# The last copy to the output, by every second row instead of by halves

## The reference, cut to what matters

```
x = x + gnn(layernorm(x), edges, ...)          # x is [2500, 512] float32
x = x + ffn(layernorm(x)[None], ...)[0]

# in ffn:
for e in range(8):
    h = gelu(xf @ W1[e] + b1[e])
    y = h @ W2[e] + b2[e]
    out = out + comb[:, e:e+1] * y             # comb is zero but for a row's two experts
```

## Time and profile before

| | |
|---|---|
| median of 3 runs | 868.01 us (867.37 to 868.9) |
| the profiled execution's own time | 863.36 us |
| its span, first to last instruction | 861.7 us |
| last copy issued (both queues) | 842.8 us |
| from issue to landing, the two transfers | 16.7 and 18.4 us |
| copied | 5.12 MB |

### The profile page before, as it was taken

The page is one execution under the profiler, slowest core; times in us unless marked ns, Lnnn a source line. Parts: engine busy times, 40 slices in busy tenths (PEclk is TensorE's granted clock), DMA queues, the critical chain, the costliest instruction groups (busy, mean ns, idle before and its releaser), DMA issues.

```text
span 861.7 us, 14833 instructions
## 1 busy us (share of the span) xinstructions
PE 696.6 (81%) x3260; PEld 553.6 (64%) x3261; DVE 457.2 (53%) x1232; ACT 415.4 (48%) x1134; POOL 457.3 (53%) x530
## 2 busy tenths in 40 slices
PE   4999355879888787879788888959889999999960
PEld 3777245657766666667676767845547787888840
DVE  5998223555555555556465555668485433333320
ACT  4443442545545554536455545618754444545430
POOL 5000575666666666666666666310105677777750
PEclk9999687998989899989999898988988999999995
DMA  5342576666666666666656666407993577777768
GB/s 197 117 155 92 156 213 164 172 188 168 186 181 174 178 177 182 186 171 183 189 166 184 176 179 179 118 27 283 334 380 127 104 131 131 135 131 135 130 91 250
DMA packets 58299, 146.96 MB, mean 171 GB/s; under 512 B 8868, under 2 KB 18708, under 8 KB 57880
## 3 DMA queue, kind: packets, MB, share of 16 engines
q0 software_dynamic: 35216, 106.84, 50.6%
q1 hardware_dynamic: 22968, 37.16, 12.3%
q10 hardware_dynamic: 80, 2.56, 1.0%
HBM read 118.17 MB, written 33.47 MB: 176 GB/s over the span
## 4 chain that ended last, share of the span: by engine, by line
PE 40%; issue 19%; DVE 11%; DMA 11%; ACT 4%; POOL 4%; POOLq 2%; DVEq 2%; another core or an unknown queue 2%; ACTq 1%; SPq 1%
PE ps L705 30%; DMA result<-y,si 8%; PE ps L659 3%; POOL rows L506 2%; DMA x_all<-in_x_dram 2%; ACT E L951 2%; ACT ps L951 2%; PE ps L844 1%; DVE Wt L1217 1%; PE ps L785 1%; DVE S L1228 1%; DVE acc L1235 1%; PE ps L755 1%; POOL xg L593 1%
## 5 line engine op out<-in xcount | busy, mean ns | idle before, releaser
L705 PE MATMUL ps<-rows,S 128*128 128x257 f32 x1556 | 383.4, 404 | 98.7 <-issue 83.9
L506 POOL DMA_INDIRECT rows<-node_table,srcT x313 | 301.8, 964 | 234.4 <-issue 83.8
L705 PEld LDWEIGHTS ps<-rows,S 128*128 128x128 f32 x1556 | 312.3, 202 | 169.6 <-issue 121.3
L951 ACT ACTIVATE E<-sdst_b,rows 128x128 f32 x389 | 124.0, 389 | 236.2 <-DVE Wt L1217 120.7
L1235 DVE TENSOR_TENSOR acc<-acc,ps 128x514 f32 x99 | 68.0, 687 | 116.1 <-remote 77.6
L1228 DVE SCALAR_TENSOR_TENSOR S<-ps,lane,Wt 128x128 f32<-128x128 f32 x389 | 109.6, 345 | 4.4 <-issue 0.8
L951 ACT ACTIVATE ps<-sdst_b,rows 128x128 f32 x313 | 96.2, 351 | 2.0 <-issue 2.0
L844 PE MATMUL ps<-W_e,xgT 128*128 x352 | 83.4, 380 | 0.0
L602 POOL DMA_INDIRECT result<-y,si x44 | 70.4, 1601 | 11.4 <-issue 7.1
L1222 DVE TENSOR_TENSOR lane<-dstT,node_id 128x4 f32 (+1 forms) x98 | 16.1, 164 | 111.5 <-issue 77.0
L844 PEld LDWEIGHTS ps<-W_e,xgT 128*128 128x128 f32 x352 | 63.4, 190 | 6.9
(11 more groups left out here) (203 smaller groups left out, 678.8 us busy)
## 6 DMA issues: line engine op xcount, KB each, us to landing
W_e<-in_L_ffn_W_dram SPq DMA_DIRECT2D x16, 512.0 KB, 8.5
node_table<-rows SPq DMA_DIRECT2D x20, 258.0 KB, 2.7
result<-acc SPq DMA_DIRECT2D x20, 256.0 KB, 2.5
xn_table<-xn SPq DMA_DIRECT2D x20, 256.0 KB, 2.2
rows<-node_table,srcT POOLq DMA_INDIRECT x313
x_all<-in_x_dram SPq DMA_DIRECT2D x19, 256.0 KB, 3.1
out_dram<-result SPq DMA_DIRECT2D x1, 2500.0 KB, 16.7
out_dram<-result ACTq DMA_DIRECT2D x1, 2500.0 KB, 18.4
```

Source lines behind the costliest of these rows:

```text
L506: nc.gpsimd.indirect_dma_start(out=rows[:, g % RING, c, :], out_offset=None, in_=table, in_offset=bass.IndirectOffsetOnAxis(ap=srcT[:, GC ...
L705: m = pe.matmul(ps_agg[q][:, a, 0:HALF], S[:, w, c, :], rows[:, r, c, a * HALF:(a + 1) * HALF], start=(c == 0), stop=(c == n - 1))
L951: m = nc.scalar.activation(e[:, c, :], sdst_b[:, bass.ds(tile * P, P)], ACT.Exp, bias=bias, scale=scale)
```

## The change

Both transfers still copy 1250 rows each, on the same queues, at the same place, behind the same waits. Before, SyncE copied rows 0 to 1249 and ScalarE rows 1250 to 2499. Now SyncE copies the even rows and ScalarE the odd ones, on both sides. A new helper makes the view, and an assert says that the number of rows is even.

```
+        def in_turn(t, half):
+
+            return t[0:N, :].rearrange("(r two) d -> two r d", two=2)[half]
...
-            sp.dma_start(out[0:N // 2, :], result[0:N // 2, :]).then_inc(st_out, 16)
+            sp.dma_start(in_turn(out, 0), in_turn(result, 0)).then_inc(st_out, 16)
...
-            act.dma_start(out[N // 2:N, :], result[N // 2:N, :]).then_inc(st_out, 16)
+            act.dma_start(in_turn(out, 1), in_turn(result, 1)).then_inc(st_out, 16)
```

More of the change, by code:

```diff
@@ L108, in gnn_moe_kernel @@
         rows = sg("rows", [P, RING, GC, ROW], F32, first)
-        assert layer_end <= top[0]
+        assert layer_end <= top[0] and N % 2 == 0
         before = top[0]
```

## The result

The changed kernel takes 874.03 us (median of 4, 873.22 to 875.84) against 867.85 us of the kernel before on the same chip (median of 4): a ratio of 1.0071, 95% interval [1.0045, 1.0096], 6.2 us slower, with 3.9 to 8.3 us as the interval. Both intervals hold the 4.9 us that the traces show in the copy itself.

What follows compares the result with a forecast made beforehand. The exposed output copy at the end was taken to decide any change: 1.3 us to first byte, 23.0 moving and 0.4 at the end make 24.7 against 18.4, so 868.0 + 6.3 = 874.3 us, range 871.0 to 880.0.

Steps and rivals of the forecast that it cites:

- The copy is wholly exposed: Output copy at the kernel's end: nothing computes beside it, so its 18.4 us, longer or shorter, changes kernel time in full.
- Ten engines, by the divisor: Output copy: 1250 rows per queue run on ten engines instead of 16, 10 being the largest divisor up to 16.
- 250 packets of 92 ns, 23.0 us: Moving time of the output copy: each shared engine carries 250 row packets at 92 ns, 23.0 us.
- The pieces given to a queue, at nothing: Output copy: 2500 pieces instead of 128 cost nothing, at 340 pieces a microsecond; at most 3.7 us for one queue.
- Issue to first byte, 1.3 us: Start of the output copy: 1.3 us from its issue until the first packet moves.
- Gaps of 0.4 us: End of the output copy: uneven finish and the way to the semaphore shrink from 1.3 to 0.4 us.
- The sum: Output copy from issue to landing: 24.7 us against 18.4, so the kernel is 6.3 us slower.
- Sixteen engines and faster: Rival for the output copy: pieces dealt to all 16 engines at a load's pace, 3.4 us sooner, 864.6 us; 7%.
- Its counterpart, memory or something else shared as the limit: Rival for the output copy: sixteen engines, but memory limits at 299 GB/s, no change, 867.2 to 868.5 us; 5%.
- Packets that wait for reading and writing in turn: Rival for the output copy: ten engines, 110 to 178 ns a packet, up to 27.8 us more, 895.8 us; 9%.
- Two engines by a power of two: Rival for the output copy: only two engines per copy, 1250 packets on each, 88 us more; 1%.

Runs made afterwards that it cites:

- long-piece kernel: Against the kernel before: the two queues copy alternate pieces of 51,200 bytes, 50 each, on ten engines; ratio 1.0047 [1.0025, 1.0069], copy 22.0 us.
- the counts of twelve to sixteen: Against the kernel before: 1236, 1246 or 1248 alternate rows per queue, remaining rows in small transfers; ratios 1.0025, 1.0011, 1.0017.
- 1248-row kernel: Against the kernel before: 1248 alternate rows per queue on sixteen engines, last four rows in two small transfers; ratio 1.0017 [1.0004, 1.0030], copy 19.3 us.
- second timing: The changed kernel timed again without edit, against the kernel before: ratio 1.0050 [1.0037, 1.0063], 4.4 us slower, copy 23.2 us.

## Why the prediction was right, step by step

- *The copy is wholly exposed.* Right. The copy's 4.9 us came through in full, in both timings' intervals, and the long-piece kernel's 3.6 us in the trace came out as 3.7 (closer than its interval, 2.0 to 5.4, can promise).
- *Ten engines, by the divisor.* Right, and now seen with five shapes: 1250 and 50 pieces on ten, 1236 on twelve, 1246 on fourteen, 1248 on sixteen, on ScalarE's queue as on SyncE's. The rule that the prediction quotes beside it from the Trainium skill ("DMA: Bandwidth & Descriptors", section "Why a DMA increments its semaphore by 16 and not by 1") holds in each. A power of two is excluded by twelve, fourteen and ten.
- *250 packets of 92 ns, 23.0 us.* The size of this term was too large. I had taken the middle between 84 ns and the 101 ns of before's own packets. The pace at ten engines is 80 ns (256 GB/s), because the 20.2 GB/s of an engine before were not its way of copying but the shared limit, as the ten-engine run with long pieces and the counts of twelve to sixteen show. Moving took 21.3 us from the first packet's start (852.1 by the packet records) to the last one's end (873.4).
- *The pieces given to a queue, at nothing.* The beginning is slower than the sum has it, by about 1 us. In 852.5:854.7 SyncE's queue alone brings 162 GB/s, 79 rows a microsecond, and ScalarE's first packet starts some 2.7 us after SyncE's. 2.7 us x (256 - 162) / 256 = 1.0 us. Whether the number of pieces causes it is not shown, and two runs speak against that as the only cause. In the 1248-row kernel SyncE's queue alone starts 256 rows in 772.3:774.2, 135 a microsecond, so 79 is not the most that it can be given. And in the long-piece kernel, with 50 pieces, SyncE's first ten packets take 2.6 us each, against 1.96 over the whole copy. My 340 pieces a microsecond came from a stretch with transfers already queued.
- *Issue to first byte, 1.3 us.* Too small by 0.4: the first packet comes 1.7 us after issue (1.4 before). The issues themselves take 0.94 and 1.65 us instead of 0.62 and 0.65.
- *Gaps of 0.4 us.* About right: 0.3 us from the last packet's end to the end of the wait. Some 0.3 us more of moving is left over that no term accounts for.
- *The sum.* 24.7 us to landing against 23.3 measured: 6.3 us forecast, 4.9 in the trace. The timed 6.2 us meet the forecast more closely than its terms deserve; the second timing gave 4.4. The mechanism is right. The packet term was 3.0 us too high (250 x 80 ns = 20.0 us), and 1.6 us that I hadn't counted took half of that back: 1.0 of slow beginning, 0.4 ahead of the first packet and 0.3 left over, less 0.1 at the end. That the errors stand against each other is luck.
- *The rivals.* Sixteen engines and faster: not what happened, and wrong even where sixteen engines are had: that kernel is 1.3 us slower than before, not 3.4 faster. Its counterpart, memory or something else shared as the limit, is what that kernel ran into. Packets that wait for reading and writing in turn, 110 ns and more: not seen; rows took 84 ns on ten engines and 103 ns on sixteen. Two engines by a power of two: excluded by the ten completions.

## What to carry to other kernels

Before a transfer on SyncE's or ScalarE's queue is given another shape, look at its outermost count as the program carries it: the largest divisor up to 16 is the number of engines that carry it, and the completion packets of the queue show it (1260 for 1250 rows means ten). Two rows of each taken out into a small transfer of their own bring the other six engines back, if not all of the time (1.3 us over before). Then ask what those engines share: copying within DRAM, twelve at 25.6 GB/s nearly reached the limit, so ten cost 4 to 5 us while sixteen instead of fourteen brought nothing measurable, and no length of packet between 8,000 and 53,248 bytes brought more than 1.5 us.

## What was unexpected of the hardware

- Copies of 2 KB rows from DRAM to DRAM average 317 to 323 GB/s on fourteen and sixteen engines, with loads at 399 to 416 on the same engines.
- The first transfer of each queue takes longer to issue when it runs on fewer than sixteen engines: 0.94 to 1.00 us on SyncE and 1.37 to 1.71 on ScalarE, with 50 pieces as with 1250, against 0.62 to 0.65 with sixteen, with 64 pieces as with 1248. The transfers issued right behind them, on sixteen engines, took anything from 0.58 to 3.93 us.
- The second of two transfers issued together starts 2.1 to 3.6 us after the first in all the kernels with two large ones, though it was issued 0.01 to 0.02 us later; before had this too (3.5 us).
